# A permute of graph edges moved out of the sorting stage and woven into the first block's edge sum, with six PSUM banks in place of eight

## The chip, the cores and the metric

The kernel runs on one core of a Trainium2 chip, as one launch. The metric is the device time of that launch in microseconds. Every engine (TensorE or PE, VectorE or DVE, ScalarE or ACT, GpSimd or POOL, SyncE or SP) has its own in-order instruction stream; they meet through semaphores only. PSUM has eight banks (`m.psum[0]` to `m.psum[7]`), each 128 x 512 float32.

## The reference

Node features `x` are 3125 x 256. Four blocks are added to `x`, each of a layer norm of `x`:

```python
edge_index = jnp.stack([src, dst])
x = x + _L0_gnn_ref(_layernorm(x), W, bias, edge_weight, src, dst)     # 50000 edges: sum of weight * (norm(x) @ W)[dst] into row src
x = x + _L0_ffn_ref(_layernorm(x)[None], ..., L0_ffn_edge_index)[0]    # gates by attention over 32768 edges, then 4 gated experts
x = x + _L1_gnn_ref(_layernorm(x), edge_index, ...)                    # 3 attention layers over the 50000 edges
x = x + _L1_ffn_ref(_layernorm(x)[None], ...)[0]                       # routed experts
```

Only index work and the first block matter here:

```python
support = input_feature @ weight
messages = edge_val[:, None] * support[edge_col]
output = jax.ops.segment_sum(messages, edge_row, num_segments=N_NODES)
return output + bias
```

Attention needs, for each of its two graphs, the edges in order of their destination, so that edges of the same 32 nodes stand together in columns of 128.

## The kernel before

The program is a list of stages. `Stage` opens a block with one instruction stream per engine and ends it with a barrier of all engines (line 1508 is the clearing of semaphores at its start). Inside a stage an engine's work stands in the order in which the helpers are called. The edges are sorted on the chip, three times:

- Graph 0 is `src`/`dst` of the first block (50000 edges, 415 chunks of 128, `NCS`). `place_edges` computes where each edge goes. `scatter_edges` (lines 425 to 440) writes the records to DRAM with 400 indirect DMAs from POOL. `merge_edges` reads them back.
- Graph 1 is the gate's (32768 edges, 256 columns in, `NCFG` = 360 columns out). Graph 2 is the attention's (50000 edges, 400 columns in, `NCF` = 504 columns out). For these `place_fine` computes places (PE counts, DVE adds up), and `permute_edges` (lines 388 to 421) moves the records with matmuls. For each column `f` DVE builds three one-hot tiles in float16 (lines 402 to 404: a 128 x `ncol` one and two 128 x 128 ones) and PE multiplies each of the two small ones with the wide one (line 420), which accumulates in banks 6 and 7 over all columns. `PERM` = 5 slots of tiles are in use at a time. At the end five DVE instructions (lines 408 to 412) unpack the banks into `lows` and `sources`.

One stage, called the scatter stage below, holds `scatter_edges`, the first `norm_rows` and `project`, and then `sort(1)` and `sort(2)`, each being `place_fine` and `permute_edges`. So DVE runs norm, projection copies, place 1, permute 1, place 2, permute 2 while POOL issues the scatter's 400 DMAs. The stage ends when both are done. The merge stage follows, and then the sum stage.

The sum stage is `sum_edges` (lines 620 to 672). All its 415 chunks are written out in the program. For each chunk `c` POOL gathers 128 rows of `table_sum` into one of 16 buffers (line 661), DVE `mark`s (line 635: a 128 x 128 tile with the weight at each edge's row), PE multiplies the two into bank `c % 8` (line 672; one float32 matmul stands in the trace as two records), and DVE `take`s the bank into the bucket's accumulator (line 641). `mark` runs 8 chunks ahead of `take`; PE waits for `taken` of 8 chunks ago before it writes a bank again; POOL waits for `summed` of 16 chunks ago. All eight banks are in use.

The gate's attention, three stages later, is the first to read `lows[0]` and `sources[0]`, which permute 1 makes.

Of the kernel before, what the change touches and what calls it, by code (L numbers as in the profile page):

```python
# [5 lines left out]
P = 128  # L6
N = 3125
D = 256
E = 50000
EG = 32768  # L10
# [4 lines left out]
PERM = 5  # L15
# [6 lines left out]
STEP = 2.0 ** 50  # L22
# [6 lines left out]
ALU = mybir.AluOpType  # L29
# [5 lines left out]
I32 = mybir.dt.int32  # L35


NCS = (E + NT * (P - 1)) // P
# [8 lines left out]
NCF = columns_sorted(E)  # L47
NCFG = columns_sorted(EG)
# [85 lines left out]
def columns_for(edges):  # L134

    return 400 if edges == E else 256
# [480 lines left out]
                nc.vector.tensor_copy(rows[:, t, 0:width], ps_h[t % TB]).then_inc(taken, 1)  # L617


def sum_edges(nc, block, m, name, table, rec, index, bucket):  # L620


    hot, summed, taken, cleared = (m.sem(f"{name}_{s}") for s in ("hot", "summed", "taken", "cleared"))
    f = m.sums
    RS, PS = len(f.rows), len(f.hot)
    landed = [m.dma_sem(f"{name}_landed{s}") for s in range(RS)]
    ps = [m.psum[s][:, 0:D] for s in range(PS)]
    part = rec.rearrange("p (c k) -> p c k", k=3)

    @block.vector  # L630
    def _(dve):
        def mark(c):
            if c >= PS:
                dve.wait_ge(summed, c - PS + 1)
            nc.vector.tensor_scalar(f.hot[c % PS][:, :], m.iota[:, :], part[:, c, 0:1], part[:, c, 2:3], ALU.is_equal, ALU.mult).then_inc(hot, 1)  # L635

        def take(c, b):
            dve.wait_ge(summed, c + 1)
            if c:
                dve.wait_ge(taken, c)  # L640
            nc.vector.tensor_tensor(m.acc[:, b, 0:D], m.acc[:, b, 0:D], ps[c % PS], ALU.add).then_inc(taken, 1)  # L641

        nc.vector.memset(m.acc[:, :, :], 0.0).then_inc(cleared, 1)
        dve.wait_ge(cleared, 1)
        for c in range(PS):
            mark(c)
        for c in range(NCS):
            if c % 4 == 0:
                n = min(4, NCS - c)
                b = nc.values_load_multi_w_load_instructions(bucket[0:1, c:c + n], [mybir.EngineType.DVE], min_val=0, max_val=NT,  # L650
                                                             skip_runtime_bounds_check_because="a bucket's number counts up to 25 buckets")[1]
            take(c, b[c % 4])
            if c + PS < NCS:
                mark(c + PS)

    @block.gpsimd
    def _(pool):
        for c in range(NCS):
            if c >= RS:
                pool.wait_ge(summed, c - RS + 1)  # L660
            nc.gpsimd.indirect_dma_start(  # L661
                out=f.rows[c % RS][:, :], out_offset=None, in_=table,
                in_offset=bass.IndirectOffsetOnAxis(ap=index[:, c:c + 1], axis=0)).then_inc(landed[c % RS], 16)

    @block.tensor
    def _(pe):
        for c in range(NCS):
            pe.wait_ge(hot, c + 1)
            if c >= PS:
                pe.wait_ge(taken, c - PS + 1)  # L670
            pe.wait_ge(landed[c % RS], 16 * (c // RS + 1))
            nc.tensor.matmul(ps[c % PS], f.hot[c % PS][:, :], f.rows[c % RS][:, :], start=True, stop=True).then_inc(summed, 1)  # L672


def attend_edges(nc, block, m, name, width, table, at_dram, nch, lows, rows_in, bucket, own_hot, starts, trip_count):
# [687 lines left out]
def memory(nc, ctx):  # L1363
    m = Memory()
# [83 lines left out]

    f = m.sums = Memory()
    f.rows = [view(D) for _ in range(16)]  # L1450
    f.hot = [view(P) for _ in range(8)]
    assert at[0] <= WORK, at[0]
    at[0] = 0
    f = m.flash = Memory()
# [57 lines left out]
def program(nc, a, y_out):  # L1512
    with ExitStack() as ctx:
        m = memory(nc, ctx)
        table_sum = nc.dram_tensor("table_sum", [NT * P, D], F32).ap()
        table_gate = nc.dram_tensor("table_gate", [NT * P, 24], F32).ap()
        table_att = nc.dram_tensor("table_att", [NT * P, D + 2 * HEADS], F32).ap()
        ends_gate = nc.dram_tensor("ends_gate", [2 * HEADS, NT * P], F32).ap()
        ends_att = nc.dram_tensor("ends_att", [2 * HEADS, NT * P], F32).ap()
        sorted_dram = [nc.dram_tensor(f"sorted{c}", [P * NCS + P, 3], F32).ap() for c in range(COPIES)]  # L1520
        xn, hidden = m.xn[:, :, :], m.hidden

        with Stage(nc, m) as block:
            setup(nc, block, m, a["x"])
        graphs = (None, (a["L0_ffn_edge_index"][1], a["L0_ffn_edge_index"][0], NCFG), (a["dst"], a["src"], NCF))

        def sort(block, k):
            key, val, nch = graphs[k]
            place_fine(nc, block, m, f"place{k}", key, val, nch, m.fine_record[k - 1], m.bucket[k][:, :], m.own_hot[k - 1][0:NS, :],
                       m.starts[k - 1][:, :], m.trips[:, k:k + 1])  # L1530
            permute_edges(nc, block, m, f"permute{k}", key.shape[0], nch, m.fine_record[k - 1], m.lows[k - 1][:, :], m.sources[k - 1][:, :])

        with Stage(nc, m) as block:
            place_edges(nc, block, m, "place0", a["src"], a["dst"], a["edge_weight"], sorted_dram, m.record, m.row, m.bucket[0][:, :])
        with Stage(nc, m) as block:
            scatter_edges(nc, block, m, "scatter", E, sorted_dram, m.record, m.row)
            normed = m.sem("norm0_done")
            norm_rows(nc, block, m, "norm0", m.x[:, :, :], xn, done=normed)
            project(nc, block, m, "sup", a["L0_gnn_weight"], D, m.xn, table_sum, after=normed)
            for k in (1, 2):  # L1540
                sort(block, k)
        with Stage(nc, m) as block:
            merge_edges(nc, block, m, "merge", sorted_dram, m.rec[:, :], m.index[:, :])
        with Stage(nc, m) as block:
            sum_edges(nc, block, m, "sum", table_sum, m.rec[:, :], m.index, m.bucket[0])
        with Stage(nc, m) as block:
            add_sums(nc, block, m, "addsum", a["L0_gnn_bias"])
            norm_rows(nc, block, m, "norm1", m.x[:, :, :], xn, square=hidden)

        with Stage(nc, m) as block:  # L1550
            project(nc, block, m, "gate", a["L0_ffn_W_gat"], 16, m.xn, table_gate, a["L0_ffn_att_src"], a["L0_ffn_att_dst"], ends_gate, keep_t=m.xt)
        with Stage(nc, m) as block:
            attend_edges(nc, block, m, "gatt", 16, table_gate, ends_gate, NCFG, m.lows[0], m.sources[0], m.bucket[1], m.own_hot[0][0:NS, :],
                         m.starts[0][:, :], m.trips[0:1, 1:2])
        with Stage(nc, m) as block:
            gate_nodes(nc, block, m, "gates", a["L0_ffn_b_gat"], a["L0_ffn_ln_gamma"], a["L0_ffn_ln_beta"])
        with Stage(nc, m) as block:
            experts(nc, block, m, "ffn0", 4, m.x, (a["L0_ffn_W1"], a["L0_ffn_b1"], a["L0_ffn_W2"], a["L0_ffn_b2"]))

        with Stage(nc, m) as block:  # L1560
            norm_rows(nc, block, m, "norm2", m.x[:, :, :], xn, square=hidden)
        layers = (("W1", "as1", "ad1", "b1"), ("W2", "as2", "ad2", "b2"), ("WN", "asN", "adN", "bN"))
        for k, (w, att_src, att_dst, b) in enumerate(layers):
            with Stage(nc, m) as block:
                project(nc, block, m, f"l{k}p", a["L1_gnn_" + w], D, m.xn if k == 0 else hidden, table_att,
                        a["L1_gnn_" + att_src], a["L1_gnn_" + att_dst], ends_att)
            with Stage(nc, m) as block:
                attend_edges(nc, block, m, f"l{k}e", D, table_att, ends_att, NCF, m.lows[1], m.sources[1], m.bucket[2], m.own_hot[1][0:NS, :],
                             m.starts[1][:, :], m.trips[0:1, 2:3])
            with Stage(nc, m) as block:  # L1570
                finish_layer(nc, block, m, f"l{k}f", k, a["L1_gnn_" + b])

        with Stage(nc, m) as block:
            norm_rows(nc, block, m, "norm3", m.x[:, :, :], xn)
        with Stage(nc, m) as block:
            turn_rows(nc, block, m, "turn")
            route(nc, block, m, "route", a["L1_ffn_Wr"], a["L1_ffn_br"], a["L1_ffn_W1"], a["L1_ffn_b1"], a["L1_ffn_W2"], a["L1_ffn_b2"])
        with Stage(nc, m) as block:
            experts(nc, block, m, "ffn1", 2, m.xn)
        with Stage(nc, m) as block:  # L1580
            norm_rows(nc, block, m, "norm4", xn, xn)
        with Stage(nc, m) as block:
            finish(nc, block, m, a["L1_ffn_gamma"], a["L1_ffn_beta"], y_out)
# [26 lines left out]
```

## Time and profile before

| | us |
|---|---|
| median of 3 runs (lowest, highest) | 4795.85 (4791.31, 4803.54) |
| the profiled execution's own time | 4785.39 |
| its span | 4783.7 |
| PE busy in the span | 3182.4 (67%) |
| DVE busy in the span | 2949.8 (62%) |
| POOL busy in the span | 2498.3 (52%) |

A busy share is a mean over stages with different limits. Where the change is made only two stages count, so the rows below are cut to those: the scatter stage from about 62 to 820 us of the span and the sum stage from about 847 to 1375 us. In a row, "idle before" is the time in which the engine did nothing just before such an instruction, with what ended it; "issue" means that nothing in the profile held it. PEclk 1.00 is 2.4 GHz and 0.50 is 1.2 GHz.

### The profile page before, as it was taken

What the parts mean: (1) busy time and instruction counts of PE and PEld (TensorE: products, weight loads), DVE (VectorE), ACT (ScalarE), POOL (GpSimd) and SP (SyncE); (2) the same over time, 40 slices, a digit from 0 to 9 for tenths busy, and PEclk for the clock granted to TensorE, in tenths of its full rate; (3) what the DMA queues carried; (4) which work ended last, traced back from release to release, by engine and by line L of the source; (5) the groups of instructions that cost most, each with busy time, mean ns of one, the idle gap of its engine ahead of it and who ended that gap; (6) DMA issues with size and microseconds to landing.
All of it is one profiled execution on the core that took longest, in us unless ns stands there. A gap on an engine that the chain in (4) does not pass through costs nothing. (4 is left out here: it accounts for less than half of the span.)

```text
span 4783.7 us, 86591 instructions
## 1 busy us (share of the span) xinstructions
PE 3182.4 (67%) x23551; PEld 1892.3 (40%) x23551; DVE 2949.8 (62%) x8769; ACT 1877.2 (39%) x6577; POOL 2498.3 (52%) x2504
## 2 busy tenths in 40 slices
PE   3677887788847554899566666566665576664293
PEld 2313211333314333677344444344443344443172
DVE  6897898655563565222466666466666376667525
ACT  0000000000004776211177776277776287776210
POOL 4777700677733776000077776177775277774100
PEclk8797899555555555999755555655555655555597
DMA  2000001333321000000244444344443433442000
GB/s 91 18 2 6 2 1 43 95 105 105 106 48 12 9 9 8 25 16 0 55 122 105 105 105 87 81 110 106 105 105 75 101 105 104 104 104 63 20 1 29
DMA packets 201216, 297.98 MB, mean 62 GB/s; under 512 B 110660, under 2 KB 140319, under 8 KB 201023
## 3 DMA queue, kind: packets, MB, share of 16 engines
q0 software_dynamic: 108656, 245.98, 20.9%
q1 hardware_dynamic: 92398, 50.07, 4.2%
q8 instruction: 74, 1.21, 0.1%
q14 instruction: 88, 0.71, 0.1%
HBM read 272.84 MB, written 23.05 MB: 62 GB/s over the span
## 5 line engine op out<-in xcount | busy, mean ns | idle before, releaser
L719 POOL DMA_INDIRECT work<-table_att,work x1368 | 1353.8, 990 | 1130.3 <-ACT work L817 714.5
L888 PE MATMUL psum<-ident,work 128*128 128x128 f32 x1656 | 559.0, 475 | 444.0 <-ACT work L841 442.6
L738 DVE TENSOR_TENSOR work<-work 128x512 f32<-128x512 f32 x414 | 288.0, 696 | 611.9 <-issue 284.6
L896 PE MATMUL psum<-work 128*32 128x65 f32 (+1 forms) x13248 | 417.8, 294 | 313.7 <-ACT work L848 280.2
L888 PEld LDWEIGHTS psum<-ident,work 128*128 128x128 f32 x1656 | 301.6, 182 | 744.4 <-ACT work L841 578.5
L661 POOL DMA_INDIRECT work<-table_sum,index x415 | 392.8, 947 | 365.1 <-SPq L1508 239.0
L841 ACT ACTIVATE work<-work 128x128 f32<-128x128 f32 x1656 | 529.4, 391 | 133.5 <-DVE work L758 132.5
L831 ACT ACTIVATE work<-psum,work 128x128 f32<-128x128 f32 x1656 | 472.4, 369 | 236.3 <-DVE work L767 230.4
L503 ACT ACTIVATE stats<-stats 128x25 f32<-128x25 f32 x5 | 1.1, 223 | 1395.2 <-DVE stats L493 1395.2
L436 POOL DMA_INDIRECT sorted<-xt x400 | 423.1, 1058 | 183.1 <-issue 121.7
L672 PE MATMUL psum<-work 128*128 128x256 f32 x830 | 433.8, 637 | 123.5 <-DVE work L635 46.2
L896 PEld LDWEIGHTS psum<-work 128*32 128x32 f32 x13248 | 330.6, 165 | 433.7 <-issue 304.4
L753 DVE SCALAR_TENSOR_TENSOR acc<-acc,work,psum 128x65 f32 (+1 forms) x1656 | 445.4, 269 | 76.9 <-DMA acc<-table_att 12.1
L880 PE MATMUL psum<-ident,work 128*128 128x128 f32 x1656 | 461.2, 434 | 39.2 <-DVE work L738 38.0
L420 PE MATMUL psum<-work 128*128 128x504 f16 (+1 forms) x1312 | 365.2, 362 | 94.8 <-DVE work L404 52.1
L719 POOL DMA_INDIRECT work<-table_gate,work x288 | 306.0, 1063 | 216.7 <-ACT work L817 129.2
L824 ACT ACTIVATE work<-iota,lows 128x32 f32<-128x32 f32 x1656 | 401.8, 333 | 0.0
L672 PEld LDWEIGHTS psum<-work 128*128 128x128 f32 x830 | 195.2, 288 | 361.8 <-DVE work L635 304.4
L880 PEld LDWEIGHTS psum<-ident,work 128*128 128x128 f32 x1656 | 295.8, 217 | 106.8 <-issue 57.1
L848 ACT COPY work<-psum 128x512 f32<-128x512 f32 x414 | 242.4, 586 | 199.0 <-PE psum L888 199.0
L641 DVE TENSOR_TENSOR acc<-acc,psum 128x256 f32 x415 | 174.9, 421 | 236.0 <-PE psum L672 234.1
L1264 PE MATMUL psum<-xt,work 128*128 (+1 forms) x960 | 267.2, 437 | 73.6 <-ACTq L1303 44.5
(292 smaller groups left out, 4362.7 us busy)
## 6 DMA issues: line engine op xcount, KB each, us to landing
work<-table_att,work POOLq DMA_INDIRECT x1368
table_att<-acc SPq DMA_DIRECT2D x75, 132.0 KB
acc<-table_att SPq DMA_DIRECT2D x12, 812.5 KB, 17.6
work<-table_sum,index POOLq DMA_INDIRECT x415, 2.7
sorted<-xt POOLq DMA_INDIRECT x400, 2.2
sorted<-work SPq DMA_DIRECT2D x8, 622.5 KB, 8.2
work<-sorted SPq DMA_DIRECT2D x8, 622.5 KB, 8.0
work<-table_gate,work POOLq DMA_INDIRECT x288
```

Source lines behind the costliest of these rows:

```text
L420: ins = nc.tensor.matmul(ps[k], row_hot[s][:, k, :], col_hot[s], start=f == 0, stop=f == fc - 1)
L436: nc.gpsimd.indirect_dma_start(out=rec_dram[s], out_offset=bass.IndirectOffsetOnAxis(ap=row[:, f:f + 1], axis=0), in_=record[:, f, :], in_ ...
L661: nc.gpsimd.indirect_dma_start(out=f.rows[c % RS][:, :], out_offset=None, in_=table, in_offset=bass.IndirectOffsetOnAxis(ap=index[:, c:c + ...
L672: nc.tensor.matmul(ps[c % PS], f.hot[c % PS][:, :], f.rows[c % RS][:, :], start=True, stop=True).then_inc(summed, 1)
L719: nc.gpsimd.indirect_dma_start(out=rows[s][:, t, :], out_offset=None, in_=table[:, 0:rw], in_offset=bass.IndirectOffsetOnAxis(ap=f.index[s ...
L753: nc.vector.scalar_tensor_tensor(acc[:, b, :], acc[:, b, :], f.fac[s][:, t:t + 1], ps_s[s % 2][:, t, :], ALU.mult, ALU.add).then_inc(taken, 1)
L824: ins = nc.scalar.activation(f.pen[s % 2][:, t, :], m.iota[:, 0:DB], ACT.Square, scale=STEP, bias=lows[:, bass.ds(q * QD + t, 1)])
L831: ins = nc.scalar.activation(f.y[s % 2][:, t, :], ps_z[s % 2][:, t * P:(t + 1) * P], ACT.Identity, bias=dst[:, bass.ds(q * QD + t, 1)])
L841: nc.scalar.activation(f.pt[s % 2][:, t, :], f.y[s % 2][:, t, :], ACT.Exp, bias=f.neg[s][:, t, 1:2]).then_inc(exped, 1)
L880: ins = nc.tensor.transpose(ps_z[s % 2][:, t * P:(t + 1) * P], f.z[s % 2][:, t, :, :].rearrange("p h d -> p (h d)"), m.ident[:, :])
L888: nc.tensor.transpose(ps_p[s % 2][:, t * P:(t + 1) * P], f.pt[s % 2][:, t, :], m.ident[:, :]).then_inc(turned2, 1)
L896: ins = nc.tensor.matmul(ps_s[s % 2][DB * h:DB * (h + 1), t, :], f.p[s % 2][:, t, DB * h:DB * (h + 1)], rows[s][:, t, h * w1:(h + 1) * w1] ...
```

## The change

Permute 1 (256 columns) leaves the scatter stage, which keeps place 1, place 2 and permute 2. Its work is written into `sum_edges`: after `take` and `mark` of chunk `c` DVE builds the columns from `due(c)` to `due(c + 1)`, which is none or one (256 columns over 400 chunks), and PE multiplies them two chunks later, behind the matmul of its chunk. The columns accumulate in banks 6 and 7, so the sum's chunks turn over six banks, and `mark` runs six ahead. At chunk 403 (`ready`) DVE unpacks. The POOL stream of `sum_edges` is as before.

```diff
-def sum_edges(nc, block, m, name, table, rec, index, bucket):
+def sum_edges(nc, block, m, name, table, rec, index, bucket, edges, nch, record, lows, sources):
...
+    fc = columns_for(edges)
+    to_row, to_col, high, low = (record[:, k, :] for k in range(4))
+    ps_moved = [m.psum[6][:, 0:nch], m.psum[7][:, 0:nch]]
+    col_hot, row_hot = [m.perm_col[s][:, 0:nch] for s in range(PERM)], m.perm_row
+    behind, ready = 2, NCS - 12
+
+    def due(c):
+        return max(0, min(fc, c * fc // (ready - behind - 1)))
...
+        def build(g):
+            s = g % PERM
+            if g >= PERM:
+                dve.wait_ge(moved, g - PERM + 1)
+            nc.vector.tensor_scalar(col_hot[s], m.iota_wide[:, 0:nch], to_col[:, g:g + 1], None, ALU.is_equal)
+            nc.vector.tensor_scalar(row_hot[s][:, 0, :], m.iota_wide[:, 0:P], to_row[:, g:g + 1], high[:, g:g + 1], ALU.is_equal, ALU.mult)
+            nc.vector.tensor_scalar(row_hot[s][:, 1, :], m.iota_wide[:, 0:P], to_row[:, g:g + 1], low[:, g:g + 1],
+                                    ALU.is_equal, ALU.mult).then_inc(built, 1)
+
+        def unpack():
+            chain = Chain(dve, steps)
+            dve.wait_ge(moved, fc)
...
             take(c, b[c % 4])
             if c + PS < NCS:
                 mark(c + PS)
+            for g in range(due(c), due(c + 1)):
+                build(g)
+            if c == ready:
+                unpack()
...
     @block.tensor
     def _(pe):
+        def move(g):
+            pe.wait_ge(built, g + 1)
+            for k in range(2):
+                ins = nc.tensor.matmul(ps_moved[k], row_hot[g % PERM][:, k, :], col_hot[g % PERM], start=g == 0, stop=g == fc - 1)
+            ins.then_inc(moved, 1)
+
         for c in range(NCS):
...
             nc.tensor.matmul(ps[c % PS], f.hot[c % PS][:, :], f.rows[c % RS][:, :], start=True, stop=True).then_inc(summed, 1)
+            for g in range(due(c - behind), due(c - behind + 1)):
+                move(g)
...
-    f.hot = [view(P) for _ in range(8)]
+    f.hot = [view(P) for _ in range(6)]
+    f.whole, f.part = view(NCFG), view(NCFG)
...
-            for k in (1, 2):
-                sort(block, k)
+            place(block, 1)
+            place(block, 2)
+            permute_edges(nc, block, m, "permute2", E, NCF, m.fine_record[1], m.lows[1][:, :], m.sources[1][:, :])
...
-            sum_edges(nc, block, m, "sum", table_sum, m.rec[:, :], m.index, m.bucket[0])
+            sum_edges(nc, block, m, "sum", table_sum, m.rec[:, :], m.index, m.bucket[0],
+                      EG, NCFG, m.fine_record[0], m.lows[0][:, :], m.sources[0][:, :])
```

## Rows read from the trace of the kernel before

**Rows 1.** Windows: length, busy time of each engine (instructions), PEclk, DMA share, GB/s

```profile
137.00:214.00 77.00, 48.80 (x424) 23.87 (x424) 69.25 (x263) 0.00 (x0) 59.31 (x59) 0.63 0.03 2
214.00:390.00 176.00, 124.64 (x512) 29.24 (x512) 175.12 (x773) 0.00 (x0) 135.46 (x134) 0.98 0.03 2
390.00:534.00 144.00, 107.68 (x826) 63.58 (x826) 99.82 (x272) 0.00 (x0) 109.70 (x113) 0.65 0.04 5
608.50:820.00 211.50, 177.20 (x592) 33.49 (x590) 210.59 (x889) 0.00 (x0) 0.18 (x1) 1.00 0.00 1
854.00:1375.00 521.00, 433.85 (x830) 195.24 (x830) 284.96 (x831) 0.00 (x0) 388.00 (x410) 0.59 0.37 104
```

**Rows 2.** Timeline, permute 1's two ends: start, duration, engine, line, operation [idle]

```profile
214.11 0.52 DVE L402 TENSOR_SCALAR work<-work,xn 128x360 f16<-128x360 f16 x1 [0.25 <-DVE starts L383]
390.23 0.39 DVE L341 MEMSET xt<- 128x400 int32 x1 [0.35 <-DVE sources L412]
```

**Rows 3.** Timeline of POOL: the scatter's last instruction

```profile
607.58 1.11 POOL L436 DMA_INDIRECT sorted<-xt  x1 [0.30 <-issue]
```

**Rows 4.** Groups of POOL in 214:390, 390:534 and 534:608: busy, mean ns | idle

```profile
L436 POOL DMA_INDIRECT sorted<-xt x134 | 136.7, 1020 | 40.8 <-issue 40.8
L436 POOL DMA_INDIRECT sorted<-xt x113 | 109.8, 971 | 34.5 <-issue 34.5
L436 POOL DMA_INDIRECT sorted<-xt x53 | 58.7, 1107 | 16.2 <-issue 16.2
```

**Rows 5.** Groups in 854:1375, the sum stage

```profile
L672 PE MATMUL psum<-work 128*128 128x256 f32 x830 | 433.8, 637 | 123.5 <-DVE work L635 46.2 <-DMA work<-table_sum,index 43.2 <-DVE acc L641 22.5
L661 POOL DMA_INDIRECT work<-table_sum,index x410 | 388.1, 946 | 124.9 <-issue 98.7 <-PE psum L672 26.2
L641 DVE TENSOR_TENSOR acc<-acc,psum 128x256 f32 x415 | 174.9, 421 | 236.0 <-PE psum L672 234.1 <-issue 0.4
L635 DVE TENSOR_SCALAR work<-iota,rec 128x128 f32<-128x128 f32 x415 | 144.5, 350 | 0.0
```

**Rows 6.** Groups by shape in 214.0:389.9, permute 1's columns

```profile
L403 DVE TENSOR_SCALAR work<-work,xn 128x128 f16<-128x128 f16 x256 | 78.8, 308 | 0.0
L402 DVE TENSOR_SCALAR work<-work,xn 128x360 f16<-128x360 f16 x256 | 77.3, 302 | 0.3 <-DVE starts L383 0.3
L404 DVE TENSOR_SCALAR work<-work,xn 128x128 f16<-128x128 f16 x256 | 76.9, 300 | 0.0
```

**Rows 7.** Timeline of DVE in the sum stage, three instructions of a catching-up stretch

```profile
861.02 0.42 DVE L641 TENSOR_TENSOR acc<-acc,psum 128x256 f32 x1
861.36 0.34 DVE L635 TENSOR_SCALAR work<-iota,rec 128x128 f32<-128x128 f32 x1
861.66 0.42 DVE L641 TENSOR_TENSOR acc<-acc,psum 128x256 f32 x1
```

**Rows 8.** Timeline of DVE: the first of permute 1's five unpacking instructions

```profile
387.89 0.53 DVE L408 CAST work<-psum 128x360 int32<-128x360 f32 x1 [0.57 <-PE psum L420]
```

**Rows 9.** Timeline, sum stage: two takes behind matmuls at 1.2 GHz, the last gather

```profile
1290.68 0.42 DVE L641 TENSOR_TENSOR acc<-acc,psum 128x256 f32 x1 [1.35 <-PE psum L672]
1291.54 0.42 DVE L641 TENSOR_TENSOR acc<-acc,psum 128x256 f32 x1 [0.17 <-PE psum L672]
...
1365.64 0.95 POOL L661 DMA_INDIRECT work<-table_sum,index  x1 [0.30 <-PE psum L672]
```

**Rows 10.** Timeline, permute 1's matmuls at 1.2 GHz and at 2.4 GHz

```profile
215.17 2.12 PE L420 MATMUL psum<-work 128*128 128x360 f16 x6 [2.38 <-DVE work L404]
384.03 0.48 PE L420 MATMUL psum<-work 128*128 128x360 f16 x2 [0.19 <-DVE work L404]
```

**Rows 11.** Timeline: POOL beside long DVE instructions, and beside permute 1's first columns

```profile
70.25 6.83 DVE L490 TENSOR_TENSOR xn<-x,stats 128x6400 f32<-128x6400 f32 x1
70.44 7.47 POOL L436 DMA_INDIRECT sorted<-xt  x1 [0.30 <-issue]
...
218.67 0.95 POOL L436 DMA_INDIRECT sorted<-xt  x1 [0.30 <-issue]
```

More of the change, by code:

```diff
@@ L617, in _ @@
                 nc.vector.tensor_copy(rows[:, t, 0:width], ps_h[t % TB]).then_inc(taken, 1)
-def sum_edges(nc, block, m, name, table, rec, index, bucket):
-    hot, summed, taken, cleared = (m.sem(f"{name}_{s}") for s in ("hot", "summed", "taken", "cleared"))
+def sum_edges(nc, block, m, name, table, rec, index, bucket, edges, nch, record, lows, sources):
+    hot, summed, taken, cleared, built, moved, steps = (m.sem(f"{name}_{s}") for s in ("hot", "summed", "taken", "cleared", "built", "moved", "steps"))
+    fc = columns_for(edges)
[5 more added lines that the diff above has]
+        return max(0, min(fc, c * fc // (ready - behind - 1)))
     f = m.sums
@@ L641, in take @@
             nc.vector.tensor_tensor(m.acc[:, b, 0:D], m.acc[:, b, 0:D], ps[c % PS], ALU.add).then_inc(taken, 1)
+        def build(g):
[9 more added lines that the diff above has]
+            dve.wait_ge(moved, fc)
+            whole, part = m.sums.whole[:, 0:nch].bitcast(I32), m.sums.part[:, 0:nch].bitcast(I32)
+            chain.next(nc.vector.tensor_copy(whole, ps_moved[0]))
+            nc.vector.tensor_scalar(part, whole, 3, None, ALU.bitwise_and)
+            chain.next(nc.vector.tensor_scalar(whole, whole, 2, None, ALU.logical_shift_right))
+            nc.vector.tensor_scalar(lows, whole, -1.0, -STEP, ALU.add, ALU.mult)
+            chain.next(nc.vector.scalar_tensor_tensor(sources, part, 1024.0, ps_moved[1], ALU.mult, ALU.add))
         nc.vector.memset(m.acc[:, :, :], 0.0).then_inc(cleared, 1)
@@ L1525, in program, with place @@
         graphs = (None, (a["L0_ffn_edge_index"][1], a["L0_ffn_edge_index"][0], NCFG), (a["dst"], a["src"], NCF))
-        def sort(block, k):
+        def place(block, k):
             key, val, nch = graphs[k]
@@ L1530, in sort @@
                        m.starts[k - 1][:, :], m.trips[:, k:k + 1])
-            permute_edges(nc, block, m, f"permute{k}", key.shape[0], nch, m.fine_record[k - 1], m.lows[k - 1][:, :], m.sources[k - 1][:, :])
         with Stage(nc, m) as block:
```

## Prediction

> **What bounds the kernel now.** I read the windows by stage first, because the change touches only two stages and the whole-span shares say nothing about those. In the scatter stage DVE is what works without a pause: 175.1 of 176 us during permute 1, 210.6 of 211.5 us from 608.5 to 820 us [rows 1]. The reader is to see that POOL, the stage's other long worker, has its last instruction at 607.6 us [rows 3] and then idles for over 200 us. So this stage's end is DVE's, and each microsecond off DVE's list there moves the end, until POOL's end is met.
>
> In the sum stage the picture is turned round. POOL has 415 gathers of 0.946 us, and before almost all of them there is 0.30 us of "issue" (124.9 us over 410), which nothing in the profile holds [rows 5]. A gather starts every 1.25 us, and 415 of these are 519 us, the stage. The 26.2 us put down to PE are pauses of the same 0.30 us, and no longer. DVE is busy 285 of 521 us and its idle time stands before `take`, ended by PE, which waited for rows or marks [rows 1, 5]. So POOL's own pace bounds the stage, and DVE has slack. The change takes work from a stage that DVE bounds and lays it beside one that POOL bounds.
>
> **Removed from the scatter stage.** From the first column of permute 1 to the first instruction of place 2 it is 390.23 - 214.11 = 176.1 us [rows 2]. It is all on the path. What follows (place 2, 144 us, and permute 2) keeps its order and lies 176 us earlier; the two loads that place 2 issues on SP move with it, behind nothing that is new. Gain: 176.1 us.
>
> **Is POOL late next there?** 100 of the 400 scatter issues lie ahead of 214 us, as 134 + 113 + 53 lie behind it [rows 4]. Place 2 then runs from 214 to 358 us and takes 113 issues along as before, so 187 are left. Beside permute 2 an issue takes 1.107 us and 0.306 us of pause, 1.41 us together [rows 4]; 187 of these are 264 us, POOL ends at 622 us, and its data lands a few us later. DVE ends at 820 - 176 = 644 us. POOL's cover of some 20 us is thin but holds: cost 0. It would fail only if an issue there took over 1.5 us, and each further 0.1 us would then cost 19 us. Place 2 follows place 1 directly; TensorE's granted clock there was a mixture (0.65) and was 0.63 in place 1 [rows 1], so I allow 5 us either way for it and take 0.
>
> **Added to DVE in the sum stage.** Back to back, `take` and `mark` together take 861.66 - 861.02 = 0.64 us [rows 7]. DVE was done with permute 1's columns 0.57 us before 387.89 us [rows 8], so a column took (387.32 - 214.11) / 256 = 0.68 us [rows 2]. The whole is 415 x 0.64 + 256 x 0.68 = 266 + 174 = 440 us. POOL needs 519 us, so DVE would be 85% occupied. A chunk with a column takes 1.32 us, 0.07 us over POOL's pace; there are never more than two such in a row, and the next chunk without one (0.64 us) gives it all back. In the other reading, where the recorded durations don't overlap, it is 415 x (0.421 + 0.350) + 256 x (0.302 + 0.308 + 0.300) = 320 + 233 = 553 us [rows 5, 6], 34 us over POOL. I take the first, since both pitches were seen on DVE itself, and keep 34 us as its upper end. Unpacking goes from 387.89 us [rows 8] to 0.35 us before 390.23 us [rows 2], 2.0 us, at chunk 403, when no columns are left and each chunk leaves DVE 0.6 us free; PE has finished the columns at chunk 401. Hidden, cost 0; without that cover 2 us.
>
> **Added waits.** `build` waits for `moved` of five columns ago, some eight chunks back. PE's `move` waits for columns built two chunks ago, while DVE is at most 0.1 us behind. Behind PE's wait stand the next chunk's matmuls, for which `take` and, 16 chunks later, POOL wait; those 16 buffers are 20 us of cover. Six banks in place of eight let DVE lag by six chunks, 7.5 us, against a lag of well under one. All of these cost 0; their upper ends are the two rivals below.
>
> **Added to PE.** Two matmuls of 128x360 float16 per column. At 2.4 GHz a pair took 0.48 us [rows 10]; beside a chunk's matmul there is room in 1.25 us. At 1.2 GHz a chunk's matmuls follow each other every 1291.54 - 1290.68 = 0.86 us [rows 9], and a pair of the permute cost at most 2.12 / 3 = 0.71 us [rows 10]. All at the low clock that is 415 x 0.86 + 256 x 0.71 = 357 + 182 = 539 us, 20 us over POOL. The sum stage's granted clock was 0.59, so mostly 1.2 GHz, with PE at 434 us of 521 [rows 1]; in permute 1 it was 0.98 with PE at 125 of 176 us. With the columns added PE has more to do, and I expect a clock between the two. I take 0 and keep 20 us.
>
> **POOL beside the columns.** The path of the sum stage is POOL, so this is the term with weight. Beside permute 1 a scatter issue took 1020 ns; undisturbed it is about 955 ns (218.67 us: 0.95) [rows 4, 11]. That is 65 ns x 134 = 8.7 us per 256 columns. I take 9 us, since it is the same three instructions on DVE as often as before. From below 0: the first columns held nothing [rows 11]. From above, 65 ns on all 401 gathers up to the last column, 26 us.
>
> The Trainium skill ("SBUF — State Buffer", section "SBUF: two separate sides") speaks against this change: VectorE and GpSimd share one pair of ports, and the one that has it holds it exclusively for its whole instruction, while descriptors written by GpSimd must wait. The trace agrees for long instructions: a scatter issue that began beside the 6.83 us instruction on DVE took 7.47 us [rows 11]. For permute 1's short ones it shows a mean of 65 ns. What that rule would do at its strictest is the last rival below.
>
> **Sum.** -176.1 + 9 = -167 us. The profiled execution took 4785.4 us and would take 4618 us. It lay 10.5 us under the median, so for the median I say 4795.85 - 167 = 4629 us.
>
> **Rivals.**
> - PE becomes the sum's bound at 1.2 GHz. For it: the clock is mostly low there, and 539 us is over 519. If the permute's pairs also break up the chunks' pitch to about 1.0 us, it is 415 + 182 = 597 us, 78 us over. Against it: PE waits 123.5 us in the stage now [rows 5], and in permute 2, with PE at 177 of 211.5 us, the granted clock was 1.00 [rows 1]. Time: 4795.85 - 176 + 20 to 78 = 4640 to 4698, say 4655 us.
> - DVE becomes the bound, with its recorded durations end to end: 4795.85 - 176 + 34 = 4654 us. Against it is the pitch in [rows 7].
> - The scatter's POOL ends last. It needs issues of over 1.5 us: at 1.6 us 14 us are lost, 4643 us.
> - The other side: POOL and the columns shut each other out. If a gather can't run while a column is built and DVE's three can't run while a gather is, every column adds its full 0.91 us to POOL's chain: 256 x 0.91 = 233 us, more than the 176 gained, and the time is 4795.85 - 176 + 233 = 4853 us. It decides from 176 / 256 = 0.69 us per column. For it: [rows 11], 7.47 us beside one DVE instruction. Against it: 256 columns of 0.91 us and 134 issues of 1.02 us are 370 us of work, and they ran side by side in 176 us [rows 1, 4].
> - The move changes nothing, since the columns just cost in the new place what they did in the old (0.69 us each): 4796 us. Against it is DVE's 236 us of idle time before `take` [rows 5].
>
> **How the numbers follow.** Forecast 72%, with a range of its own from 4612 (no hold on POOL, 5 us for place 2's clock) to 4646 us (26 us for POOL). PE 13%, DVE 7%, scatter end 3%, nothing changed 2%, shut-out 3%. The range of 4610 to 4668 us takes in the forecast, the scatter end, DVE's case and the nearer half of PE's. A measurement of this kernel tells about 0.3%, 14 us, from no change; all but the last two cases are faster by more: faster 0.95, within 0.02, slower 0.03.
>
> **What would show it.** Place 2's first instruction at about 214 us and permute 2's end near 644 us; POOL's last scatter issue near 622 us, ahead of that. In the sum stage gathers with "issue" alone in front and a mean under 1.0 us, a stage of 520 to 545 us, DVE busy about 500 us by its recorded durations, and `take` still waiting for PE. I am wrong if the gathers wait for PE by more than 0.30 us (PE or DVE bounds), if their mean is above 1.05 us (port), or if DVE idles at the end of the scatter stage while POOL works.

## The result and the profile after

The changed kernel took 4611.76 us (median of 4 runs, 4606.91 to 4617.73), the kernel before 4798.34 us beside it. The ratio is 0.9614, 95% interval 0.9602 to 0.9626. Forecast were 4629 us, 167 us less than before; it was 186.6 us less, and the median lies only 1.8 us inside the lower end of the range (4610 us). Two later comparisons, told below, give 173.8 and 177.3 us.

The profiled execution took 4617.73 us, 167.7 us less than the one before (4785.39), while my sum said 167. That agreement is partly luck, as the terms show.

First the windows of the changed kernel (length, busy time of each engine with its instructions, PEclk, DMA share, GB/s), cut as [rows 1]: place 2, permute 2, and the sum stage without its head and tail.

```profile
216.00:366.00 150.00, 112.22 (x828) 64.26 (x826) 101.57 (x273) 0.00 (x0) 114.02 (x119) 0.65 0.04 5
366.00:653.00 287.00, 240.60 (x800) 46.65 (x800) 285.22 (x1205) 0.00 (x0) 203.68 (x184) 0.99 0.02 2
690.00:1185.00 495.00, 345.98 (x1307) 174.55 (x1307) 448.21 (x1565) 0.00 (x0) 374.66 (x396) 0.98 0.36 105
```

The same length of the sum stage in the kernel before:

```profile
863.00:1358.00 495.00, 414.81 (x790) 184.97 (x790) 271.18 (x790) 0.00 (x0) 374.51 (x396) 0.60 0.35 105
```

Both issue 396 gathers in 495 us. DVE went from 271 to 448 us busy, and PE, with more matmuls, is busy for less time (415 to 346 us), because its granted clock rose from 0.60, a mixture nearer 1.2 GHz, to 0.98, nearly all at 2.4 GHz.

Now the timeline where the stages meet: place 2's first instruction (answering to [rows 2]), POOL's last scatter issue (to [rows 3]), the last of DVE in the scatter stage, and the first DMA of the merge.

```profile
218.17 0.39 DVE L341 MEMSET xt<- 128x400 int32 x1 [0.36 <-DVE starts L383]
...
624.34 1.11 POOL L436 DMA_INDIRECT sorted<-xt  x1 [0.30 <-issue]
...
651.55 0.67 DVE L412 SCALAR_TENSOR_TENSOR sources<-work,psum 128x504 int32<-128x504 int32 x1
...
652.85 1.30 SPq L452 DMA_DIRECT2D work<-sorted  x3
```

DVE still ends the scatter stage. In this execution everything before it had taken 4.1 us longer (the scatter began at 68.0 us instead of 63.9), so the merge begins 167.7 us earlier than the 820.5 us of before, and counted from the scatter's first issue 171.7 us earlier. Nearly all of the other 4.4 us of the 176.1 are place 2's: from its first instruction to its last before the columns (line 383) it is 365.3 - 218.2 = 147.1 us, where it was 533.0 - 390.2 = 142.8. Its granted clock is 0.65, as before, so the clock does not explain that.

The sum stage's groups (busy, mean ns | idle before), 690 to 1185 us, answering to [rows 5, 6]. L693 is the gather, L650 `take`, L644 `mark`, L656 to L658 a column's three tiles:

```profile
L693 POOL DMA_INDIRECT work<-table_sum,index x396 | 375.2, 948 | 120.6 <-PE psum L710 98.4 <-issue 22.2
L650 DVE TENSOR_TENSOR acc<-acc,psum 128x256 f32 x399 | 165.7, 415 | 46.8 <-PE psum L710 43.5 <-issue 0.3
L644 DVE TENSOR_SCALAR work<-iota,rec 128x128 f32<-128x128 f32 x398 | 159.5, 401 | 0.0
L656 DVE TENSOR_SCALAR work<-work,xn 128x360 f16<-128x360 f16 x256 | 95.5, 373 | 0.0
L658 DVE TENSOR_SCALAR work<-work,xn 128x128 f16<-128x128 f16 x256 | 81.8, 319 | 0.0
L657 DVE TENSOR_SCALAR work<-work,xn 128x128 f16<-128x128 f16 x256 | 78.5, 307 | 0.0
```

The reader is to see three things. First, the gather takes 948 ns (946 before) with 120.6 / 396 = 0.305 us of pause; that more of these pauses are now put down to PE changes nothing, since the longest of them is 0.307 us. Second, `take` still waits for PE, so DVE has slack. Third, DVE's records grew: `mark` from 350 to 401 ns, the first tile from 302 to 373. From the first gather to the first addition after the sum it is 1208.7 - 679.7 = 529.0 us, against 1375.5 - 847.6 = 527.9.

Where the longer DVE records come from, the timeline tells. A gather began at 803.60 us and took 0.95, to 804.55. Another began at 799.84 and lasted to 800.79.

```profile
800.39 0.48 DVE L656 TENSOR_SCALAR work<-work,xn 128x360 f16<-128x360 f16 x1
800.79 0.30 DVE L657 TENSOR_SCALAR work<-work,xn 128x128 f16<-128x128 f16 x1
...
804.08 0.52 DVE L644 TENSOR_SCALAR work<-iota,rec 128x128 f32<-128x128 f32 x1
804.33 0.35 DVE L656 TENSOR_SCALAR work<-work,xn 128x360 f16<-128x360 f16 x1
```

The `mark` of 804.08 us ends at 804.60, just behind its gather. That is so of every one: between 690 and 1185 us 173 of the 398 marks start 0.42 to 0.65 us into a gather, and all 173 end 40 to 60 ns after that gather's end. Their records are 478 ns in the mean, the others' 341 ns. In the kernel before it was the same for 24 of 415 marks (480 and 342 ns). So a `mark` that starts in the later part of a gather is held until the gather is over, and the change only made more of them start there. A held record need not delay what follows: the first tile starts 0.25 us after the held `mark`, as after any other. Where the first tile is held, the second does start later (0.40 us after it at 800.39, where an unheld one takes 0.22). From first to second tile it is 0.292 us in the mean, against 0.228 in permute 1: 16 us over 256 columns, inside DVE's slack.

### The profile page after: what moved, and what is told of

Its sections match the earlier page's. It is cut to its first block and busy times, and to the rows that moved or that the text cites. A ratio compares the mean times of both kernels' runs of the same rounds, so it can differ in the third digit from the quotient of the medians.

```text
span 4616.0 us, 86590 instructions
## 1 busy us (share of the span) xinstructions
PE 2996.3 (65%) x23551; PEld 1853.8 (40%) x23551; DVE 2952.3 (64%) x8769; ACT 1879.7 (41%) x6577; POOL 2507.5 (54%) x2504
## 5 line engine op out<-in xcount | busy, mean ns | idle before, releaser
L436 POOL DMA_INDIRECT sorted<-xt x400 | 435.8, 1089 | 187.2 <-issue 121.6
L693 POOL DMA_INDIRECT work<-table_sum,index x415 | 393.4, 948 | 180.3 <-PE psum L710 99.3
L710 PE MATMUL psum<-work 128*128 128x256 f32 x830 | 284.0, 431 | 184.6 <-DMA work<-table_sum,index 110.1
L798 DVE SCALAR_TENSOR_TENSOR work<-work 128x512 f32<-128x512 f32 x414 | 285.3, 689 | 17.5 <-ACT work L871 17.0
L807 DVE TENSOR_REDUCE work<-psum 128x512 f32 (+1 forms) x414 | 285.9, 691 | 2.3
L420 PE MATMUL psum<-work 128*128 128x504 f16 x800 | 240.6, 385 | 44.4 <-DVE work L404 2.5
```

Of the source, the lines that this page charges most:

```text
L436: nc.gpsimd.indirect_dma_start(out=rec_dram[s], out_offset=bass.IndirectOffsetOnAxis(ap=row[:, f:f + 1], axis=0), in_=record[:, f, :], in_ ...
L693: nc.gpsimd.indirect_dma_start(out=f.rows[c % RS][:, :], out_offset=None, in_=table, in_offset=bass.IndirectOffsetOnAxis(ap=index[:, c:c + ...
L807: nc.vector.tensor_reduce(self_max[:, bass.ds(q * (2 * QD), 2 * QD)].rearrange("p (t k) -> p t k", k=2)[:, :, 1], ps_z[k % 2].rearrange("p ...
```

## The experiments

**The change again, six banks alone, no permute 1, columns built twice.** These four ran side by side.

The edit of the second, in the kernel before:

```diff
-    f.hot = [view(P) for _ in range(8)]
+    f.hot = [view(P) for _ in range(6)]
```

Of the third, in the changed kernel (it leaves permute 1 out; `fill` writes valid numbers that are not the reference's):

```diff
-            for g in range(due(c), due(c + 1)):
-                build(g)
             if c == ready:
-                unpack()
+                fill()
...
-            for g in range(due(c - behind), due(c - behind + 1)):
-                move(g)
```

Of the fourth, in `build` of the changed kernel (`...` inside a line stands for operands left out):

```diff
+            spare = m.work[:, 6000 + 400 * s:6400 + 400 * s].bitcast(F16)
+            nc.vector.tensor_scalar(spare[:, 0:nch], ..., to_col[:, g:g + 1], None, ALU.is_equal)
+            nc.vector.tensor_scalar(spare[:, 400:528], ..., to_row[:, g:g + 1], high[:, g:g + 1], ALU.is_equal, ALU.mult)
+            nc.vector.tensor_scalar(spare[:, 528:656], ..., to_row[:, g:g + 1], low[:, g:g + 1], ALU.is_equal, ALU.mult)
             nc.vector.tensor_scalar(col_hot[s], ...)
```

> The changed kernel once more, in five rounds beside the kernel before. In the two profiled executions the change took 4785.4 - 4617.7 = 167.7 us off, but the medians differ by 186.6 us, more than the 176.1 us that permute 1 took. Theory A (the removed 176 us is all there is, the columns cost the sum stage about nothing, the rest is scatter between executions): the difference of medians comes to 168 to 180 us, ratio 0.9625 to 0.9650. Rival B (the change gains something besides permute 1's own time, such as a higher TensorE clock in stages around it): 182 us or more again, ratio 0.962 or less.

> The kernel before with one edit: the sum turns over six PSUM banks in place of eight, permute 1 stays in the scatter stage. If the banks are only cover (theory A: gathers start every 1.25 us whatever DVE does), the sum stage stays at 528 us and the ratio is 1.000 within 0.002. If two banks fewer make PE wait for DVE (rival), POOL's pauses before gathers pass 0.30 us and the stage grows by 5 us or more, ratio 1.001 or more.

> The changed kernel with permute 1 left out altogether: no columns are built or moved in the sum stage, and lows and sources of graph 1 are filled with valid numbers that are not the reference's by three DVE instructions. It is the most that any placing of permute 1 can gain. Theory A (POOL paces the sum, the columns are free beside it): the same time as the changed kernel within 3 us, gathers of 946 ns; the clock in the sum stage falls back from about 0.97 to about 0.6 with no effect on the time. My prediction's term (POOL held by the columns) would make this kernel 9 us faster than the changed one. Rival (DVE or PE binds in part): 15 us or more faster.

> The changed kernel, in which DVE builds each column's three tiles a second time into spare memory just ahead of the real ones. That adds 256 x 0.68 = 174 us of DVE work to the sum stage and nothing to PE or POOL. Theory A (take and mark 0.64 us, a column 0.68 us, POOL's pace 519 us): DVE needs 266 + 2 x 174 = 614 us for the columns' 400 chunks and the rest, so DVE is the bound and the stage grows from 529 to about 615 to 625 us, 90 us in all. If DVE's true cost is that of its recorded durations (0.77 and 0.91 us) it is 320 + 466 = 786 us, 255 us more. It also tells whether gathers are held by columns: with DVE never idle, as in permute 1, their mean goes to about 1010 ns if continuous columns hold POOL, and stays at 948 ns if a gather of the sum is not held.

Measured, in us and as ratio to the kernel before (5950.45): the change 5794.93 (0.9735, 0.9721 to 0.9748), six banks 5951.97 (0.9999, 0.9990 to 1.0008), no permute 1 5778.35 (0.9706), built twice 5808.51 (0.9760). All, the kernel before too, took 24% longer than in the first pair. The waits of the changed kernel there, 60 to 1200 us (engine, line, releaser: total, times, longest), show how:

```profile
DVE acc L617 <- remote: 290.2, 19, 16.4
ACT work L558 <- remote: 266.1, 17, 16.4
DVE xn L199 <- remote: 124.4, 1, 124.4
```

These are waits for which the profile finds no releaser on this core ("remote"), and they are up to 124 us long while POOL issues indirect DMAs. Permute 2, which there ran after POOL's last issue, took 286 us as ever (850 to 1136 us, DVE busy 284.8). What slowed the rest the runs don't tell; each of the three series of experiments ran on another chip, and whether that is the cause is not shown. So of these four only two things are used. Six banks in place of eight cost nothing measurable even there. And each added step cost something there (columns 16.6 us, built twice 13.6 us more); that this comes of the long waits is my reading. The question was then put again.

**The same three without that disturbance, and a version past the change.** The last one takes the last 40 (`REST`) of permute 2's 400 columns into the sum as well. They accumulate in banks 4 and 5, so the sum turns over four banks, and DVE unpacks both graphs there. Its edit, besides tables of columns for both graphs:

```diff
+REST = 40
 def permute_edges(...):
-    fc, ncol = columns_for(edges), nch
+    fc, ncol = columns_for(edges) - REST, nch
-    ps = [m.psum[6][:, 0:ncol], m.psum[7][:, 0:ncol]]
+    ps = [m.psum[4][:, 0:ncol], m.psum[5][:, 0:ncol]]
...
-    f.hot = [view(P) for _ in range(6)]
+    f.hot = [view(P) for _ in range(4)]
```

> The changed kernel again. In the first four experiments everything, the kernel before too, took some 24% longer than in the pair of the prediction, with waits on semaphores of 5 us and more wherever indirect DMAs ran; there the change took 155.5 us off, not 186.6. If these runs come to about 4800 us before, the question of the first pair is asked again: 168 to 180 us off if the columns cost nothing and permute 1's 176 us is all, 182 or more if something else was gained. If they come to 5950 us again, 150 to 160 us off.

> The changed kernel without permute 1 (no columns built or moved, graph 1's lows and sources filled with valid numbers that are not the reference's). With semaphores quick: POOL paces the sum, so the time is that of the changed kernel within 3 us, with gathers of 946 ns in both and the clock in the sum stage down to about 0.6. With my prediction's term it would be 9 us less than the changed kernel. Slowed as in the first four it was 16.6 us less, because each PE and DVE step there waited longer; that again if the runs are slow.

> The changed kernel with every column's tiles built a second time into spare memory, 174 us more of DVE work in the sum stage. With semaphores quick, by pitches (0.64 us for take and mark, 0.68 us a column): DVE needs 266 + 348 = 614 us, the stage grows from 529 to 615 to 625 us, ratio to the kernel before 0.979 to 0.982. By recorded durations 786 us, ratio above 1.01. In the slowed runs it added only 13.6 us, as the stage was 619 us long already. If columns without a pause hold POOL, the gathers' mean goes to about 1010 ns.

> Past the change: of permute 2's 400 columns the last 40 are woven into the sum as well (296 columns over 400 chunks). Their banks 4 and 5 keep the partial sums over the merge stage, so the sum turns over four banks. Scatter stage: 40 x 0.705 = 28 us less for DVE, which then ends 2 us after POOL's last issue or ties with it, so 24 to 28 us off. Sum stage: DVE by pitches 266 + 296 x 0.69 = 470 us of 519, POOL stays the bound, 0 to 5 us more (unpacking twice, four banks of cover). In all 20 to 28 us faster than the changed kernel. If four banks are too few or DVE's true cost is nearer its recorded durations, the sum grows by 20 us or more and nothing is won.

| beside 4789.32 us before | us | ratio | 95% |
|---|---|---|---|
| the change | 4615.56 | 0.9667 | 0.9624 to 0.9710 |
| no permute 1 | 4615.83 | 0.9641 | 0.9624 to 0.9657 |
| built twice | 4690.55 | 0.9803 | 0.9784 to 0.9822 |
| 40 columns of permute 2 too | 4594.47 | 0.9600 | 0.9582 to 0.9617 |

The change's interval is wide because one of its four executions took 4652 us. Leaving permute 1 out is worth nothing measurable beyond weaving it in: in the sum stage it is nearly free, 529.1 us here with it and 528.6 without (1201.6 - 673.0). Its windows without permute 1 (683 to 1178 us) have the old clock and the same number of gathers:

```profile
683.00:1178.00 495.00, 403.99 (x797) 184.32 (x795) 273.46 (x799) 0.00 (x0) 374.58 (x396) 0.62 0.36 105
```

So the clock's rise from 0.62 to 0.98 comes with the columns, and the stage's time hardly differs between the two, as POOL paces both.

Built twice, the slack is gone. The window of its whole sum stage, and its gathers from 687 to 1260 us:

```profile
676.90:1290.50 613.60, 365.92 (x1342) 211.56 (x1342) 608.60 (x2372) 0.00 (x0) 400.86 (x415) 0.87 0.32 89
```

```profile
L697 POOL DMA_INDIRECT work<-table_sum,index x398 | 384.5, 966 | 189.5 <-PE psum L714 122.3 <-issue 67.2
```

DVE is busy 608.6 of 613.6 us, and 614 us was what the pitches gave (266 + 348). The recorded durations would have given 786 us. Here POOL does wait: 189.5 / 398 = 0.48 us before a gather, up to 2.55 us. Its mean of 966 ns is that of two kinds: half take 946 ns or less, and 90 of 398 take 1.0 us or more.

The version with 40 more columns is faster than the change by 21.1 us (17.7 us by the next series' ratio for the change, 0.9637). Its sum stage stays at 529.3 us. What limits it is the scatter stage, where now POOL comes last (the timeline):

```profile
617.82 0.30 DVE L407 TENSOR_SCALAR work<-work,xn 128x128 f16<-128x128 f16 x1
618.10 0.96 POOL L433 DMA_INDIRECT sorted<-xt  x1 [0.30 <-issue]
627.62 4.21 SPq L449 DMA_DIRECT2D work<-sorted  x8
```

The merge's first DMA came 8.6 us after the end of POOL's last scatter. That is not late data: the last scatter's data had landed 1.15 us after that end, 2.1 us after its start. What comes between is an instruction of POOL's own sequencer, with which it closes the stage:

```profile
L1555 POOLq DRAIN  x1: 6753/6753/6753, 620.5 to 620.5; - x1
```

From 620.5 us it takes 6.75 us, to 627.2. The kernels before and after have it too, with the same 6753 ns (from 610.1 and from 626.9 us), hidden behind DVE there. What it waits for is not shown.

**A third measurement of the change, the columns crowded, and 90 more columns.** Edits: none; `return max(0, min(fc, c))` in `due`; `REST = 90`.

> The changed kernel a third time beside the kernel before, in five rounds. The first pair gave 186.6 us, the second undisturbed one 173.8 us with a wide interval. With permute 1's 176 us alone: ratio 0.9635 to 0.9655. If the first pair's ratio of 0.9614 comes again, something besides permute 1 is gained.

> The changed kernel with the columns crowded forward: one per chunk in chunks 0 to 255 and none after, in place of 256 spread over 400. In each of the first 256 chunks DVE then has 0.64 + 0.68 = 1.32 us of work against POOL's 1.25 us, on top of the 7 us by which it starts late, so its lag grows to 7 + 256 x 0.07 = 25 us. The 16 gather buffers cover 20 us less some 3 us for a gather to land. If the cover is what decides, POOL is held up by about 8 us in that stretch, and the time is 5 to 10 us over the changed kernel's; if the even spread didn't matter, 0 to 2 us. If waiting for POOL costs each column more than its pitch, as the longer DVE records of the woven columns suggest (a mark 401 ns for 350, a first tile 373 for 302), the lag grows by 0.2 us a chunk and the stage by 35 us or more.

> As the version with 40 columns of permute 2 in the sum, with 90. There the scatter stage already ended with POOL's issues (618 us, and its data 8 us later), so 50 columns less free DVE 35 us earlier, and that only lets POOL's last 25 issues run at 1.26 us in place of 1.41: 4 us. The sum stage: 266 + 346 x 0.69 = 505 us of DVE work in 519. If pitches hold, POOL stays the bound and it is 2 to 4 us faster than with 40; if the slack is used up before that, by the 44 us that DVE's records are longer in the woven sum, it is 15 to 40 us slower.

Beside 4787.53 us before, the change took 4610.28 us (0.9637, 0.9621 to 0.9653), crowded 4615.04 us (0.9644, 0.9630 to 0.9658), 90 more columns 4592.59 us (0.9594, 0.9581 to 0.9607).

The change is back at 177.3 us. Crowded, the difference in time is not clear of noise, but the profile shows a longer sum stage: 1207.9 - 674.6 = 533.3 us. From 695 to 1000 us DVE had no pause at all, busy 305.0 of 305 us, and POOL's group there is

```profile
L693 POOL DMA_INDIRECT work<-table_sum,index x241 | 232.3, 964 | 73.5 <-issue 47.5 <-PE psum L710 25.9
```

The pause is 0.305 us as ever, so POOL was never kept waiting for a buffer. The gathers themselves are longer, 964 for 946 ns in the mean, and 241 x 18 ns are 4.3 us, the whole loss. But it is not spread evenly: six gathers of 1.1 to 2.0 us hold 3.0 of the 4.3 us, and the median gather grew only to 952 ns. My account of a lag of 25 us and a cover of 20 was wrong: DVE did 243 chunks with a column in the 305 us, 1.255 us each, not 1.32. That is POOL's own undisturbed pace of 1.25 us, so hardly any lag builds up. The 90 columns are no better than the 40 (0.9594 and 0.9600, intervals overlapping): POOL's last issue came at 617.9 us, as with 40, though DVE's last column was built at 580 us, and the sum stage took 531.2 us, 2 us more. POOL bounds the scatter stage now.

## Why the prediction was right, point by point

- **Removed, 176.1 us.** Right in size. From the scatter's first issue to the merge's first DMA it was 756.6 us before and is 582.4 and 582.8 us in the two later profiles of the change, 174 us less. The medians gave 186.6, 173.8 and 177.3 us in three comparisons, and the version without permute 1 gives 4789.32 - 4615.83 = 173.5. The 186.6 of the first pair did not come again, so that the forecast missed it by 20 us is no fault of a term that I can name. From the first addition after the sum to the end of the span, where both kernels are the same, the profiled executions took 3408.2 us before, 3407.3 after, 3403.4 and 3398.0 in the two later ones of the change, 3417.9 in the crowded one. Executions differ by up to 20 us in code that nothing touched. That another cause added to the first pair's 186.6 is not shown, and not excluded.
- **Place 2's clock, allowed 5 us, taken as 0.** Place 2 was 4.3 us longer in the first profiled execution and 1.2 and 1.1 us longer in the two later ones (144.0 and 143.9 us). The granted clock was 0.65 in the first and 0.67 in the others, so the 4.3 us are within the allowance, but not of the cause that I allowed for.
- **POOL late in the scatter stage.** Its last issue came at 624.3 us where I had 622. The data landed soon after, as I had said. What I had left out is POOL's closing DRAIN of 6.75 us: with it POOL was done at 633.6 us, against 652.2 us for DVE's last instruction, so the cover was 18.6 us, near my "some 20" for another reason. With 40 columns less it was gone, as the count said it would be.
- **DVE in the sum stage.** Counting by pitches was right: the doubled columns landed on 613.6 us for 614, and the reading by recorded durations (786 us) is refuted. The hit is a little lucky, since the 613.6 hold the stage's head and tail too. Crowded, a chunk with a column took 1.255 us for my 1.32, so the 440 us were some 17 us too many.
- **POOL beside the columns, +9 us.** This is the step that failed. The gathers went from 946 to 948 ns, 396 x 2 ns = 0.8 us, and the sum stage from 527.9 to 529.0 us (529.1 and 529.3 later). I had carried over 65 ns from a stretch in which DVE never paused and the DMA was a scatter. DVE's pauses are part of the answer at most: with DVE gapless in the sum stage the mean came to 964 ns crowded (the median to 952) and 966 ns built twice, 18 and 20 ns, not 65. Why three quarters of the scatters beside permute 1 took 1.0 us or more (99 of the 133 that began there) stays open. The other side of it I had not looked at. In the woven sum the delay is found on DVE: its records grew by 398 x 51 ns for `mark` and by 256 x (71 - 1 + 19) ns for the tiles (L656, L657, L658), 43 us in all, of which some 16 us moved the start of a following instruction, all inside its slack. This growth does not depend on pauses either. In the crowded version DVE never paused, and its records are long too, 422 ns for `mark` and 352 to 353 ns for the tiles (350 and 300 to 308 in the kernel before), while the tiles start every 0.22 us as ever. What decides for a `mark` in the woven sum is where in the gather it starts, as shown above. The rule of the Trainium skill that I weighed ("SBUF — State Buffer", "SBUF: two separate sides") says that whichever starts first holds the shared ports for its whole instruction and the other is blocked; the page says this of DVE instructions in a 2-port mode or with two SBUF inputs, and no trace here tells whether these are. The trace agrees in that held marks end with their gather (173 of 173), but not in that every overlap holds: marks that start up to 0.35 us into a gather keep their 341 ns.
- **Unpacking, waits and six banks, 0.** The unpacking ran from 1189.1 to 1191.3 us beside gathers. Six banks alone gave 0.9999, though only in the disturbed series. Undisturbed, four banks did not hold the sum either (529.3 us).
- **PE at the low clock, up to 20 us.** Did not come. I expected a granted clock between 0.59 and 0.98; it was 0.98.
- **In the forecast signs**, DVE busy about 500 us was off (467.8 us in the stage): I had added the columns' recorded durations to 285 us, but the windows count records that overlap only once.

The total of 167 us fitted the profiled execution because of the 9 us for POOL only 1.1 us came, and the rest was made up for by 4.1 us ahead of the scatter and 4.4 us in the scatter stage. That is luck: neither came again in that size in the later profiles.

## What to carry to other kernels

Find two stages with different bounds, and move work from the engine that bounds the one into its slack in the other; count that slack by start-to-start pitches and not by recorded durations, which overlap. Spread the moved work so that the engine keeps its pauses: without gaps on DVE a gather took 18 to 20 ns more in the mean, with them 2 ns. Stop where the second-longest engine of the emptied stage comes last, and count what it does after its last DMA: here 40 columns more were worth 18 to 21 us and the next 50 nothing.

## What was not expected of the hardware

- The sum stage, with one 128x256 float32 matmul every 1.25 us and no pause of PE over 1.4 us, had a granted clock of 0.60. With two 128x360 float16 matmuls added in two chunks of three it went to 0.98, and PE's busy time fell by 69 us in 495 although it ran 65% more matmuls.
- A `mark` on DVE that starts 0.42 to 0.65 us into a gather issued by POOL ends 40 to 60 ns after that gather, without exception in the profiles counted (24 in the kernel before, 173 in the changed one, 50 with columns built twice). Its record grows to as much as 577 ns for 341. In the changed kernel the first tile starts 0.257 us after a held `mark` and 0.256 after another.
- POOL closed the scatter stage with a DRAIN of 6.75 us after its last scatter, though the data had landed 1.15 us after that scatter's end.
- In one series the stages with indirect DMAs held waits of up to 124 us, 24% on the whole time, for reasons that the records don't show; a 155.5 us gain was measured there, with the same sign and near the same size.
